# A sixteen-batch transformer layer: the experts' base product and the router as three products of float32r halves

## What is computed

```python
scale = 1.0 / np.sqrt(np.float32(weight.shape[0]))
ys = y * scale
d = jax.lax.rsqrt(jnp.einsum('bi,io->bo', ys * ys, weight * weight) + EPS)
out = jnp.einsum('bsi,io->bso', Efou * ys[:, None, :], weight) * d[:, None, :]
...
logits = jnp.einsum('bsd,ed->bse', x, Wg) + bg
scores = jax.nn.softmax(logits, axis=-1)
topv, topi = jax.lax.top_k(scores, TOP_K)
w = jnp.sum(jax.nn.one_hot(topi, E, dtype=x.dtype) * topv[..., None], axis=-2)
base = jnp.einsum('bsd,fd->bsf', x, Wi)
lora_low = jnp.einsum('bsd,erd->bser', x, A)
lora = jnp.einsum('bser,efr->bsef', lora_low, B)
h = jax.nn.relu(base[:, :, None, :] + lora)
expert_out = jnp.einsum('bsef,df->bsed', h, Wo)
out = jnp.einsum('bse,bsed->bsd', w, expert_out)
```

## Time and profile before

| | before |
|---|---|
| median of 3 runs | 1182.61 us |
| lowest, highest | 1180.33, 1185.35 us |
| span of the profiled execution | 1179.4 us |
| TensorE matmul busy | 1119.6 us, 95% |
| TensorE weight load busy | 804.4 us, 68% |
| VectorE busy | 862.7 us, 73% |
| ScalarE busy | 678.5 us, 58% |
| GpSimd busy | 241.2 us, 20% |

### The profile page before, as it was taken

How to read it: one execution, slowest core, us unless ns; L and a number is a source line. 1 busy time by engine, 2 the same in 40 slices (tenths; PEclk the granted TensorE clock), 3 DMA queues, 4 the chain that set the end, 5 groups by cost and what they waited for, 6 DMA issues and landing times.

```text
span 1179.4 us, 32772 instructions
## 1 busy us (share of the span) xinstructions
PE 1119.6 (95%) x13168; PEld 804.4 (68%) x13168; DVE 862.7 (73%) x3425; ACT 678.5 (58%) x1415; POOL 241.2 (20%) x336
## 2 busy tenths in 40 slices
PE   6879869999999999999999999999999999999998
PEld 3545545777677677777777677777767777777776
DVE  6899978978878887967767966967477895552433
ACT  1567757567765756577564756567474745434231
POOL 2222022042113230131203221022203221210111
PEclk9989989999999999999999999999999999999999
DMA  9410100001000001010000101000001000000000
GB/s 332 138 59 15 37 16 16 24 24 47 25 16 29 17 14 55 3 43 28 29 16 11 38 2 34 15 20 15 9 13 34 16 17 19 21 2 20 3 19 19
DMA packets 27353, 38.59 MB, mean 33 GB/s; under 512 B 3536, under 2 KB 21328, under 8 KB 27200
## 3 DMA queue, kind: packets, MB, share of 16 engines
q1 hardware_dynamic: 25296, 34.29, 9.0%
q10 hardware_dynamic: 1904, 2.20, 0.6%
HBM read 31.79 MB, written 4.29 MB: 31 GB/s over the span
## 4 chain that ended last, share of the span: by engine, by line
PE 73%; DVE 10%; ACT 8%; issue 4%; POOL 3%; DMA 1%; ACTq 0%; DVEq 0%; POOLq 0%
PE psg L455 44%; PE psq L455 16%; PE pso L455 7%; PE psg L458 6%; ACT PQ L1450 3%; POOL M L1797 2%; DVE nm L992 1%; DMA QK<-in_w 1%; ACT M L1450 1%; ACT JA L1461 1%; DVE JD L1005 1%; ACT QK L1450 1%; DVE U L989 1%; DVE R L989 1%; DVE lp L983 1%
## 5 line engine op out<-in xcount | busy, mean ns | idle before, releaser
L1450 ACT ACTIVATE PQ<-psq 128x2048 f32<-128x2048 f32 x112 | 210.3, 1877 | 60.7 <-PE psq L455 60.1
L1822 POOL TENSOR_TENSOR R<-R,rhoT 128x256 f32<-128x256 f32 x128 | 92.8, 747 | 402.3 <-ACT R L1450 402.3
L455 PE MATMUL psq<-QK 32*128 32x128 f32 (+5 forms) x3360 | 128.6, 304 | 1.7 <-DMA QK<-in_w 1.7
L455 PE MATMUL psg<-zT,WiT 128*128 128x256 f32 x480 | 114.5, 381 | 2.1 <-DVE R L989 1.9
L455 PEld LDWEIGHTS psq<-QK 32*128 32x128 f32 (+2 forms) x3360 | 97.3, 166 | 25.7 <-issue 18.4
L455 PE MATMUL pso<-PQ,Vg 128*32 128x256 f32 (+2 forms) x2048 | 109.6, 345 | 3.9 <-ACT PQ L1450 2.4
L455 PE MATMUL psg<-WoT,R 128*128 128x256 f32 x480 | 108.8, 381 | 0.8 <-DVE R L989 0.8
L992 DVE TENSOR_REDUCE nm<-psq 128x16 f32<-128x2048 f32 (+1 forms) x48 | 92.8, 1932 | 20.8 <-PE psq L455 20.0
L1450 ACT ACTIVATE R<-psg 128x512 f32<-128x512 f32 x60 | 35.8, 596 | 119.6 <-PE psg L455 119.4
L455 PEld LDWEIGHTS psg<-WoT,R 128*128 128x128 f32 x480 | 89.1, 190 | 15.0 <-issue 2.4
L455 PEld LDWEIGHTS psg<-zT,WiT 128*128 128x128 f32 x480 | 86.8, 190 | 15.0 <-DVE R L989 2.9
(11 more groups left out here) (236 smaller groups left out, 2278.9 us busy)
## 6 DMA issues: line engine op xcount, KB each, us to landing
bcB<-ada_rows SPq DMA_DIRECT2D x16, 384.0 KB, 3.4
bcA<-ada_rows SPq DMA_DIRECT2D x15, 384.0 KB, 3.4
X<-in_x SPq DMA_DIRECT2D x16, 256.0 KB, 3.0
XR<-in_x SPq DMA_DIRECT2D x16, 256.0 KB, 2.7
out<-XR SPq DMA_DIRECT2D x15, 256.0 KB, 2.1
QK<-NMT SPq DMA_DIRECT2D x96, 4.0 KB
...
```

The lines of the kernel that those rows point to most:

```text
L455: return e.matmul(o, lhsT, rhs, start=start, stop=stop, skip_group_check=True)
L1450: return e.activation(o, i, func, **kw)
L1822: e.tensor_tensor(R4, R4, rhoT[:, :], ALU.mult).then_inc(*pool_moe.mark(b, f"r{f}{j}"))
```

## The change

**Halves.** WiT becomes two tiles of type float32r: WiH holds Wi as that type keeps it, WiL what is left of Wi. POOL makes them once, from a staging copy of Wi that now lies in R2; likewise wrH and wrL from wrt. For z, ScalarE's copy goes to zH (float32r), in place of zT, and VectorE makes zL as z times d minus zH, one instruction for each half. Each product of z and a weight becomes three: H with H, L with H and H with L. The product of the two low halves is left out.

**Waits.** The router waits for zL as well as zH, and the bank of z is free only when VectorE has made zL. In batch 0 it waits for wrL, and the first base step for WiL. ReLU results go to R2, whose staging copy is read out by then.

**Set-up.** The masks and B are staged in R2 too, so SP waits until TensorE has read w_ada before it loads the masks. POOL has six more instructions. The program's dynamic DMA scratch is set to 1024.

**Order.** All five strings of `ORDER` are new; a row of each is shown in the diff, and the places that matter below.

```diff
 ORDER = {
     "PE": [
-        "A*An*qqqq******hh*a**aa*aaanaaooqqqqnoohhqqaqqaaanaaahaqhooaqqaqaaoaaoaNahooFFhanaaqoaaoaaqqaqoopppppphh",
+        "AA***nqqqq*****hh*a***aaaaaaanooqqqqonohqhqaqqaaaanaqaahhqoaoqaqaaaoaoaaNhooFhFanaaqaoqoaaqqaapoopppppmh",
...
     "SP": [
-        "nwxxwxx*****AAAnNn*nnNnxnmNxnmNewxNnmxNnmexwNnmNexwnmewxNnNmexwnmewNnmNewnmewNmewNmewNmNewmewmewmewee",
+        "**xx*AnxA**nnxnAN*nnxnwNmNnxmNxNewwnxmmenNwxNnxmeNwnmxeNwnNmexnwmeNwnmNenwmewNmewNmNewmNewmewmewmewee",
     ],
...
-        WiT = sb("WiT", [128, 2, FF])
         WoT = sb("WoT", [128, 8, D])
+        WiH, WiL = (sb(n, [128, 2, FF], F32R) for n in ("WiH", "WiL"))
         wrt = sb("wrt", [128, 2, 20])
+        wrH, wrL = (sb(n, [128, 2, 20], F32R) for n in ("wrH", "wrL"))
...
-        zT = sb("zT", [128, 2, 256])
+        zH, zL = (sb(n, [128, 2, 256], F32R) for n in ("zH", "zL"))
...
-        wi, wj = WiT.rearrange("p c n -> p (c n)"), WoT.rearrange("p c n -> p (c n)")
+        wi, wj = R2.rearrange("p f n -> p (f n)"), WoT.rearrange("p c n -> p (c n)")
+        WiT = R2.rearrange("p (c k) n -> p c (k n)", c=2)
...
                         for c in range(2):
-                            mm(ps[:, 256 * j:256 * j + 256], WiT[:, c, f0:f0 + 128], zT[:, c, :], c == 0 and j == 0, False)
+                            o, r = ps[:, 256 * j:256 * j + 256], slice(f0, f0 + 128)
+                            mm(o, WiH[:, c, r], zH[:, c, :], c == 0 and j == 0, False)
+                            mm(o, WiL[:, c, r], zH[:, c, :], False, False)
+                            mm(o, WiH[:, c, r], zL[:, c, :], False, False)
...
-                bank = take(pg, ("z", b), act_moe.at(b, "z1"))
+                bank = take(pg, ("z", b), dve_moe.at(b, "z1"))
...
                 w.wait_ge(*act_moe.at(b, "z1"))
+                w.wait_ge(*dve_moe.at(b, "z1"))
+                if not b:
+                    w.wait_ge(*pool_late.at(0, "wrL"))
                 for t in range(2):
                     for c in range(2):
-                        last = mm(bank[:, 20 * t:20 * t + 20], zT[:, c, 128 * t:128 * t + 128], wrt[:, c, :], c == 0, c == 1)
+                        o, tok = bank[:, 20 * t:20 * t + 20], slice(128 * t, 128 * t + 128)
+                        mm(o, zH[:, c, tok], wrH[:, c, :], c == 0, False)
+                        mm(o, zH[:, c, tok], wrL[:, c, :], False, False)
+                        last = mm(o, zL[:, c, tok], wrH[:, c, :], False, c == 1)
...
+                for oc in range(2):
+                    w.wait_ge(*act_moe.at(b, "z1"))
+                    if b:
+                        w.wait_ge(*pe_moe.at(b - 1, "a3"))
+                    stt(zL[:, oc, :], pg.where["z", b][:, 256 * oc:256 * oc + 256], dT[:, oc, b:b + 1], zH[:, oc, :], ALU.mult,
+                        ALU.subtract)().then_inc(*s.mark(b, f"z{oc}"))
+                    yield
                 w.wait_ge(*pe_moes[b].at(b, "rv"))
...
-                    act(zT[:, oc, :], bank[:, 256 * oc:256 * oc + 256], ACT.Copy,
+                    act(zH[:, oc, :], bank[:, 256 * oc:256 * oc + 256], ACT.Copy,
...
+                def halves(name, H, L, W):
+                    e.tensor_copy(H, W).then_inc(*pool_late.mark(0, f"{name[:2]}H{name[2:]}"))
+                    w.wait_ge(*pool_late.at(0, f"{name[:2]}H{name[2:]}"))
+                    e.tensor_tensor(L, W, H, ALU.subtract).then_inc(*pool_late.mark(0, f"{name[:2]}L{name[2:]}"))
+
+                w.wait_ge(*loads["wrt"])
+                halves("wr", wrH[:, :, :], wrL[:, :, :], wrt[:, :, :])
+                for c in range(2):
+                    yield
+                    w.wait_ge(*loads["WiT"])
+                    halves(f"Wi{c}", WiH[:, c, :], WiL[:, c, :], WiT[:, c, :])
...
                 yield
+                w.wait_ge(*pe_ada.at(0, "r"))
                 load(e, "mf", mf, A["masks"])
...
-    nc = _bacc.Bacc("TRN2", target_bir_lowering=False, num_devices=1)
+    nc = _bacc.Bacc("TRN2", target_bir_lowering=False, num_devices=1, dynamic_dma_scratch_size=1024)
```

More of the change, by code:

```diff
@@ L10 @@
 BF16 = mybir.dt.bfloat16
+F32R = mybir.dt.float32r
 I32 = mybir.dt.int32
@@ new lines @@
+        "mohomaaaamaNaFnFqqqqaakooknhkkkqhwkawowwopwppwapwpepqemqeNmqFmaFaeamaeeaeeaehekheekeneeeoeeNkkkFFwkpowww",
+        "apwpppwopaoqwqmNqqmFFmapaampapeaakenhkeoqkkkhqokewwwwaweeaoepopwpemewemqeeqemeaeeeamaepaeppkaaeknhNqhFFo",
+        "eokkqkakwqowawwowpNpwpwmeqFmeFeameeaenemaaeeaapeeeoeeehkopkhpkkeokoewqekawqwwawpppwqwmeeqemaeemeeamaeeae",
+        "eeeeeNaakhFpFnoopkhpqokkkeoekaNewwFaaFwwawqppqwpweemeqeemaeemeeaenmaeaeeeehhkoepokpeokkkowekpwawqqwawppw",
+        "pwmeqeemeeqeameaeemaaeeeeeeNaaFnooFhkhqkeqqoekkkpqoewkaNpwwaawpwpnpewapaewmeFemeFeempeeaeheeamaeeeokohpk",
@@ new lines @@
+        "fFfFFfFoFofFhFfFoFfFofFoFffnofnfFofofnfnoFFofnfnnfqgggggfggfggfgooggqgfgggfgqgfgfgfggfgfgqfgfgfqffffofof",
+        "offfqfqffqoqfofoqfffopfqfoqfoqfofofqPoPqPoPPoPhPmPoPoPohPPhPmPsPPooPPmPsfPPPfPPPPPPPhPPfPfPfpPPPPPfPfPfP",
+        "PPfffspfffffffmNNNNfNnNnNFnnnfnfFFFFnfFqqFfFFFfFFqqqFFFfqgqogoqqoqqogqqqqnhgoongnosggogoonogggnnghgofgog",
+        "gohgggngoqgoffggowgwwwwgwwfwgoowfffwfffffffffpffffffffNffffwfshsfffNffqfPNNPPqseeNmPPNeqPePPPPemeNePePes",
+        "PeeqFPePemeeeePFeqPpeqeFqPFeqPeqqPFPqFPPPqPFPeqmFqPFPFFeFhFPFPPPePePPFPhPhPPPPPPegeeggggggggeggggggggoNg",
@@ new lines @@
+        "egngNgnggogNNNNNggpFwFwnFoowFwwFowFoFwowFoFoFoooFohonwFnwnoFFoFopggnggggggoggoggggfgqgggqwgggmgqfggqffmf",
+        "NNNqfNgNsfgmNqNFFFfFqqFmFfFFfFFFqfFqfqfqFqnnfFfqFfgfqghgfnshpggsnshegefpeeneoeeegggnfgfgnefggefeoefeqfee",
+        "ggeegffeggegqoofooeowwowewowoewewoweoogooowogewpfegqoofffgsgfhffffffmffwfffemfefsffqfffqffgfqfsqffepfffP",
+        "PPPmqPgPPPPPPPqqmPPPqPPPPqPPqePPPeqPPPqPPPPPPPPPPPPPPPsPhpheennNnNnNnhnNNNnqNFsFFoeoFFsoFohFFFoFFFoFoFoF",
+        "ooqoooeogoqwooweqgwggwewpwwgwgoogewggwgegfNefgegeegfggNeffgfesfegegeNsegwNeNgeggeemeggeqNNgeFffmFqFfqqmF",
@@ new lines @@
+        "pqeqFfFFqqqFFeFnFnFFqFmnFefffeggpnofgnsfgggpqoghfggeseggffgoffoffgfnhohoooogoghogooofoffgogfonoofegewqfe",
+        "fefgefwffgfgefgffewwfwesefwqefwefwfgfeffefwfefffffwffeefefefeefPPeqePqeewPPmPPPPqPPgmPqqPePPPPpmPPqPPePP",
+        "PqPqPPePqPPPeqPPPqPgPPmPPPPPqPeqhnpNNNeeNNNhhNFFooFFoooFnoFFnnoFnoFooFooonFsFoFFosooFnhgqgoggopggggeggeg",
+        "gggegeNggggweggweeggNwegefewNNgegNNwNFwFwwFfseswfFwqffFqFeefFeefFfeFeqfefpefFeeFewmqFFFeFqeefmmqqeqpeeff",
+        "qnqnfqqgqfgfqgffmfhhfgfhffnfesggnenogofoonfoooogfoofooogooogfgogeepsoeoeegswewfeefggwwffgwffffefnfewfwwe",
@@ new lines @@
+        "fgffqgffeefqeffffefefwfwefffffgfePPhgPgegPPPgPPPeweqePgPPmeeqPPgPpPPPemPPPeemPPPPPPPPqPPePqPPPPqPPqqqmPP",
+        "qPqPPqesNNNNNqNeqgehnNFnhnhoonooFFnFnoFFoFoFonFoooFohqFooFooFoFFqeqqegqgoggeoqggegeeggewgqfqeqewefggepwf",
+        "eqfeweegNwqqgwegwgfwqeefegffegsfgefweqfwpngegepggNgfngwnNNmNNNfffefngnefmFfqFeFhFpmFefFFFnpFFFFFFffemFff",
+        "fgfghhgegeooooogfgoooogfoogoogooohgfgngogofgfggogggfeeffqgfffeqegweefewfefffefwfwfqfewfewfqwgfewgfefffee",
+        "efqgfewwfefffefpeeqefgPPPgPPwPqmPPeePPPPPPmPPPPqPPPePPPmPPPPPqeqPPPePqPPPqqPPPmePPPPeepNqNqhhNNeNNNhFFFo",
@@ new lines @@
+        "oFoFnooFoonoFFnFFnFonooonooonFoFFoFqgggwwggwwogowwwgeeweggegegewggfgwgegfqgffeggegffpgeeegegheffeefffwge",
+        "ggqqeefeefefpNNmeffemeNqemefpfeqqqNqqqfqNfqqempqffhNffNeeoooeohooefhoooeoeeFoeeooefooeooeeeeffeefFFeFoFw",
+        "owheeffwFFefwewFfffwfewfFffweFwFfFfffFFffffFfffeffefwfgemfeffmfffPwPePgPPPmgPPPPPPPPPePPgPgpPPPPPPePgPPg",
+        "PggPgPgPPgPgPgggPpPmPggPPgPgggPgPgPeggeoNooNoNNNooNoNoFoooFoFoFFFFFoFoFFFoFoFFeeggooggpfegeegggeffggfeff",
+        "fgeewffwffwNfwfwewfwefNwefgwgefwfegefffgefNfgNeegfgeNegfNgegegfggNfffwfPgmPgPpPFPFeFeFFPmPFeFFeFmePPPFmF",
@@ L945, in moe @@
                     yield
-                    first(b, "WiT", "WoT")
+                    first(b, "WoT")
                     if not b:
                         w.wait_ge(*dve_late.at(0, "Bst"))
+                        w.wait_ge(*pool_late.at(0, "WiL1"))
                     take(pg, ("ps", b, f), dve_moe.at(b, f"th{f}"))
```

86 lines of the change are left out of this document (29 added, 57 removed).

## The result

| | before | after |
|---|---|---|
| median of 4 runs | 1182.59 us | 1209.68 us |
| lowest, highest | 1180.33, 1185.35 us | 1208.84, 1214.07 us |
| span of the profiled execution | 1179.4 us | 1212.3 us |
| mean granted clock of TensorE | 0.991 | 0.976 |
| idle of TensorE (span less matmul busy) | 59.8 us | 91.9 us |

The ratio is 1.0239, 95% interval 1.0211 to 1.0267: 27.1 us slower, where 17.6 us faster was forecast and the range ended at 1179 us. The profiled execution of the changed kernel is the slowest of its four (1214.07 us); the other three have a mean granted clock of 0.982 to 0.983.

A forecast was written before the change was run, and what follows sets the result against it. TensorE was taken to bound the kernel in the middle. Base product -24.7, router +2.4 and last batch +1.4 us gave -20.9, less 15% -17.8, so 1165 us, range 1151 to 1179 us.

The forecast's parts named there:

- TensorE is full there: Middle of the program: TensorE, busy 398.0 of 400 us, sets the time, so work taken from it shortens the program.
- Even starts: Base-step instructions in the middle start evenly, 216 ns apart; taken as the sign that TensorE is full.
- 15% off: Whole sum: -20.9 us cut to -17.8 us because shorter base steps cover less of other engines' work.
- Base steps: Base product: twelve float32r instructions of 112 ns for eight of 216, 0.39 us less in each of 64 steps, -24.7 us.
- Rival D: Base product: a float32r column costs as much as a float32 one, +55 us, 1240 us with the router; chance 0.09.
- Router: Router: twelve instructions for eight, priced by their weight loads at 1.01 us for 0.86, +2.4 us (-2.2 to +6.7).
- zL at nothing: Making zL on VectorE: 14 us more work there, its latency covered by TensorE's other work in 15 batches, cost nothing.
- The last batch: Last batch: no cover, router starts 0.95 us later, net about zero, so a correction of +1.4 us to the other terms.
- Set-up: Start of the program: GpSimd's split of Wi, masks and copies cost nothing; without cover, 3.6 us late once.
- New order: Step order on all engines: some microseconds either way near the start, with some 6 to 10 us possible on top.
- Rival C: Router waits for VectorE's zL: 1180 us if half do (chance 0.08), 1196 us if all (0.04); VectorE as bound, 1197 us.
- TensorE stays above 98% busy in the middle: Middle of the new trace: a sign that the forecast holds, TensorE above 98% busy over fewer microseconds.

The follow-up runs named there:

- e13: The kernel before with half of the base product left out, 55 us less work on TensorE, order unchanged: 1164.82 us, ratio 0.9866.
- e11: The changed kernel in its own order without the making of zL, the third product reading zH in its place: 1206.12 us.
- e12: The kernel before, order unchanged, with two more VectorE instructions a batch (14 us in all) into a tile nobody reads: 1188.61 us, ratio 1.0053.
- e5: The changed code in the step order of the kernel before, GpSimd's two steps that split Wi standing together: 1200.47 us, ratio 1.0158.
- e10: As e5, with Wi split by ScalarE and VectorE in place of GpSimd: 1194.27 us, ratio 1.0102.
- e2: The code of the kernel before in the new step order, without the zL and splitting steps: 1201.85 us, ratio 1.0164.

## Why the prediction was wrong, point by point

- **"TensorE is full there, and what is taken from it shortens the program unless another engine is then late."** The step that failed. Even starts and 398.0 of 400 us show that TensorE waits for nobody, not that the others have slack. Here they have none in many places: results arrive just as TensorE comes to them, like the maximum above. The condition "unless another engine is then late" was the rule, and I took 15% off for it; e13 says 68%. VectorE's idle quarter, 294 of 400 us busy, was taken as slack, but it lies in other places than the waits.
- **Base steps, -24.7 us.** The mechanism held. The distance was 117 ns for 112, a step 0.33 us shorter for 0.39: -21 us of TensorE's time, within the bounds. Rival D is out. The promised 108 to 114 ns were missed by 3.
- **Router, +2.4 us.** Undersized: 112 ns an instruction, so +7.7. Its upper bound was +6.7. A float32r load takes 188 to 201 ns in the rows and repeats as a float32 one does, so the middle between float32 and bf16 was the wrong choice.
- **zL at nothing.** Right about TensorE's waits, too low in the price. TensorE waits 3.9 us for it in all, 1.9 of it in the last batch, so 2.0 outside, within the 3 that I promised; e11 puts the whole price at 3.6 us. In the old order VectorE's time is charged by itself (e12), which the sum left out because "no queue of it overflows". There, where nothing covers it in the last batches, zL costs 14.3 us. "Without that cover it is 1.0 us a batch" was right for the wait (1.14 to 1.18 us in three routers of e5), but the sum had no term for the clock behind it, 8.5 us.
- **The last batch, +1.4 us.** Too low. Forecast with its other terms was a batch of the same length; from the product with w2c (at 1154.58 us before, 1184.14 in the changed kernel) to the end it takes 28.2 us for 24.8. The router came 0.9 us later, as forecast, after a wait of 1.93 us for zL. What was missing is again the clock: the row below shows half of it granted for 6.9 us, 3.4 us of work, and the matmuls of the router and of most of the first two base steps start 213 ns apart, where they started 112 and 117 apart in the middle.

```profile
1188.00:1194.90 6.90, 6.83 (x32) 6.86 (x33) 3.52 (x19) 0.21 (x1) 0.00 (x0) 0.51 0.01 2
```

- **Set-up, nothing.** Wrong by 6.2 us in the old order (e10 against e5) and by 7.4 in the new (lag over e2). The contingency that I named, 3.6 us late once by the queue on GpSimd, happened too: the UO step behind the first piece starts 2.5 us later than in e2. What I had not seen is that VectorE stands still beside GpSimd (2.31 us in place of 0.15), which the prediction had no term for. The Trainium skill's page cited above (SBUF — State Buffer, SBUF: two separate sides) says so, and I weighed other pages but not that one.
- **New order, "some microseconds either way", 6 to 10 to gain.** The second step that failed, by sign and size: +19.3 us with the old code, 13.6 of them by the start and some 6 by the rest. This is the largest piece of the miss. I had the strings and the listing of both orders, and priced neither end. VectorE's first rows, with batch 1's statistics ahead of the end of batch 0's preparation, were to be read there without any run. A rival with this mechanism was missing from the list.
- **Rival C** came nearest. The form in which I put it, the router waiting for zL, is refuted by 3.9 us of waits. Its other form, VectorE as the bound and 1197 us, was right in kind: half of its added time comes through (e12), though no engine is the bound all along. TensorE's waits for VectorE did grow by 39 us, but 29 of them are in e2 too, so the new order made them and not the added work. The Trainium skill's warning (Perfetto Trace Analysis, Identifying the Most-Contended Engine) not to judge TensorE by matmul busy time was sound here; the even starts, by which I set it aside, answer another question.
- **The sum after the fact.** Order +19.3; the split +7.4 (lag); zL +3.6 (e11, its VectorE time included); the products -13.3 x 0.32 = -4.3 (an estimate, the rate taken over from the old order). That is 26.0 of 27.1 us, though the split's size is from one trace and zL's is uncertain by itself. The clock is inside these figures. The mean granted clock is 0.982 to 0.983 in three of the four runs of the changed kernel and 0.987 to 0.990 in e2, which is some 15 us more at 1.2 GHz, 7 us of work. Not all of that need be on the path. In runs of the kernel before alone, 1180.0 us goes with 0.993 and 1187.1 with 0.984.

One sign that the prediction named deceives: "TensorE stays above 98% busy in the middle" came true, 393.1 of 400 us, in a kernel that is 2.4% slower.
